# Stream mixing by 32x32 tiles on TensorE, with one reordering on ScalarE and one on VectorE

## The reference, cut to what matters

```python
x = x + attention(layernorm(x))
x = x + autocorrelation(layernorm(x), ctx, ctx)        # FFTs over the 128 tokens, 9 best lags per channel
x = x + ffn(layernorm(x))

def ffn(x):                                            # n = 4 streams of C = 256 channels per token
    x_norm = x * rsqrt(mean(x * x) + RMS_EPS)
    H_res  = sinkhorn(x_norm @ W_res.T + H_res_base)   # a 4x4 matrix per token, 50 iterations, tau 0.1
    H_pre  = softmax(x_norm @ W_pre.T + H_pre_base);  H_post = softmax(x_norm @ W_post.T + H_post_base)
    H_res  = (1 - g) * I + g * H_res                   # g = sigmoid(gate)
    y      = einsum('btnc,btn->btc', x_streams, H_pre) @ W_branch
    return einsum('btij,btjc->btic', H_res, x_streams) + einsum('btc,btn->btnc', y, H_post)
```

## Time and profile before

| | us |
|---|---|
| three runs | 1181.81, 1184.62, 1187.58 |
| the profiled execution | 1182.99 |
| its span, first to last instruction | 1181.20 |
| TensorE busy | 1020.6 (86% of the span) |
| VectorE busy | 904.2 (77%) |
| ScalarE busy | 611.9 (52%) |
| GpSimd busy | 488.6 (41%) |
| mean granted clock of TensorE | 0.941 of 2.4 GHz |

### The profile page before, as it was taken

How to read it: one execution, slowest core, us unless ns; L and a number is a source line. 1 busy time by engine, 2 the same in 40 slices (tenths; PEclk the granted TensorE clock), 3 DMA queues, 4 the chain that set the end, 5 groups by cost and what they waited for, 6 DMA issues and landing times. The chain is left out here.

```text
span 1181.2 us, 23560 instructions
## 1 busy us (share of the span) xinstructions
PE 1020.6 (86%) x7954; PEld 775.4 (66%) x7954; DVE 904.2 (77%) x2830; ACT 611.9 (52%) x1801; POOL 488.6 (41%) x721
## 2 busy tenths in 40 slices
PE   5899999999999999999966999999998988722538
PEld 4687777877777777778755677777676665411325
DVE  6786687666876667866554787788999999899993
ACT  6644455444555435554455677777766654310314
POOL 0723443333433334332342666667666653202212
PEclk9999999999999999999979999999999999755769
DMA  9111011111011110111032222243223311119406
GB/s 377 47 61 44 33 45 60 60 42 49 29 60 60 56 45 19 60 60 44 26 110 107 90 77 94 86 125 94 76 80 97 110 41 41 41 45 358 115 1 179
DMA packets 47236, 95.73 MB, mean 81 GB/s; under 512 B 5952, under 2 KB 30400, under 8 KB 47168
## 3 DMA queue, kind: packets, MB, share of 16 engines
q1 hardware_dynamic: 46880, 94.65, 24.1%
q10 hardware_dynamic: 288, 0.26, 0.1%
HBM read 64.48 MB, written 27.26 MB: 78 GB/s over the span
## 5 line engine op out<-in xcount | busy, mean ns | idle before, releaser
L696 POOL TENSOR_TENSOR prob_G<-prob_G,rl 128x512 f32<-128x512 f32 x96 | 99.7, 1040 | 246.5 <-DVE rl L570 246.5
L436 ACT ACTIVATE prob_G<-prob_G,negm 128x128 f32<-128x128 f32 x384 | 148.8, 390 | 83.9 <-DVE negm L512 83.9
L291 PE MATMUL ps_qkv<-w_hi,xT_hi 128*128 128x512 f32 x384 | 156.4, 407 | 12.5 <-DVE prob_G L581 8.6
L292 PE MATMUL ps_qkv<-w_lo,xT_hi 128*128 128x512 f32 x384 | 151.2, 394 | 0.0
L293 PE MATMUL ps_qkv<-w_hi,xT_lo 128*128 128x512 f32 x384 | 151.1, 393 | 0.0
L365 PE MATMUL ps_qkv<-wo_hi,aT_hi 128*128 128x512 f32 x256 | 107.8, 421 | 0.0
L366 PE MATMUL ps_qkv<-wo_lo,aT_hi 128*128 128x512 f32 x256 | 101.9, 398 | 0.0
L367 PE MATMUL ps_qkv<-wo_hi,aT_lo 128*128 128x512 f32 x256 | 101.9, 398 | 0.0
L508 DVE TENSOR_TENSOR prob_G<-ps_s,mask 128x512 f32<-128x512 f32 x96 | 64.9, 676 | 44.3 <-PE ps_s L274 43.8
L291 PEld LDWEIGHTS ps_qkv<-w_hi,xT_hi 128*128 128x128 f32 x384 | 72.9, 190 | 37.8 <-issue 15.9
L537 DVE TENSOR_TENSOR xT_lo<-ps_t,xT_hi 128x512 fp32r<-128x512 f32 x16 | 11.1, 691 | 94.9 <-ACT xT_hi L475 94.9
(11 more groups left out here) (290 smaller groups left out, 2763.5 us busy)
## 6 DMA issues: line engine op xcount, KB each, us to landing
xin<-in_x SPq DMA_DIRECT2D x16, 512.0 KB, 3.4
xres<-in_x SPq DMA_DIRECT2D x16, 512.0 KB, 5.5
x<-xres SPq DMA_DIRECT2D x16, 512.0 KB, 2.7
c_xin<-x SPq DMA_DIRECT2D x16, 512.0 KB, 5.5
c_cin<-in_ctx SPq DMA_DIRECT2D x16, 512.0 KB, 4.8
c_b_xres<-x SPq DMA_DIRECT2D x16, 512.0 KB, 3.3
rows_x<-c_row SPq DMA_DIRECT2D x64, 128.0 KB, 2.3
m_xm<-rows_x SPq DMA_DIRECT2D x16, 512.0 KB, 8.1
```

Source lines behind the costliest of these rows:

```text
L291: nc.tensor.matmul(ps_qkv[:, n, :], xT_hi[:, k, :], w_hi[:, k, cols], start=k == 0, stop=False)
L292: nc.tensor.matmul(ps_qkv[:, n, :], xT_hi[:, k, :], w_lo[:, k, cols], start=False, stop=False)
L436: r = nc.scalar.activation(prob(g)[:, j, :], prob(g)[:, j, :], ACT.Exp, bias=negm[:, h:h + 1], accum_out=lsum[:, h:h + 1])
L696: nc.gpsimd.tensor_tensor(prob(g), prob(g), rl[:, g * GROUP:(g + 1) * GROUP].rearrange("p (j o) -> p j o", o=1).to_broadcast([P, GROUP, T] ...
```

## The change

- **Tiles.** A group of mixing is now eight tokens and four streams, 32 lanes. `branch_part` and `row_part` become sixteen matmuls each of 32x32, on the four row strips and four column strips of the array, still with 256 moving columns. `post_diag` and `diag` have 128 elements per lane and row where they had 128 and 512, one GpSimd instruction per row each. A PSUM bank belongs to a row strip.
- **Constants.** `select` needs sixteen matmuls instead of four, with a quarter of the columns each; its matrices `sel` grow from 256 KB to 1 MB, and `place` (256 KB) and `fold_own` are new. `copies` is one instruction of 128 lanes.
- **Transfers.** A finished row goes out to `rows_x` in one transfer instead of four, in its natural order; it is loaded back in four transfers per row (32 lanes, pieces of 1 KB) instead of one (128 lanes of 4 KB). `TOKENS` is 8.
- **ScalarE's order.** Chain a's coefficients are copied and its rows 0 to 4 taken out ahead of chain b's first logs, row 5 behind them; chain c's second logs stand behind row 9 instead of row 8; rows 11 and 12 are now shared with VectorE too (`SHARED` = 11).
- **Bodies 8 to 14.** The first half of the residual is taken between the fourth and fifth pick (`residual_amid`). In bodies 8 to 13 the squares of the row move from the body's end to between the two key spectra of the next body (`squares_late`).

```diff
+        def residual_amid(b):
+            return isinstance(b, int) and 8 <= b < B - 1
+        def squares_late(b):
+            return isinstance(b, int) and 8 <= b < B - 2
@@ autocorrelation, sync
-                    for g in range(NS):
-                        lanes = slice(g * W, (g + 1) * W)
-                        sp.dma_start(rows_x[b - 2].rearrange("(j t) g c -> g t j c", j=NS)[g],
-                                     row[par][lanes, 0:D].rearrange("p (j c) -> p j c", j=NS)).then_inc(row_out[par], 16)
+                    sp.dma_start(rows_x[b - 2], row[par][:, 0:D]).then_inc(row_out[par], 16)
@@ autocorrelation, scalar
+            def row_squares(m):
+                act.wait_ge(x2_bias_done, m + 1)
+                nc.scalar.activation(squares[:], x2[:], ACT.Square, bias=x2_bias[:], scale=1.0 / D ** 0.5,
+                                     accum_out=x2_var[:]).then_inc(x2_sq_done, 1)
                 if near:
                     key_spectrum(0, f_b)
+                    if isinstance(b, int) and squares_late(b - 1):
+                        row_squares(b - 1)
                     key_spectrum(1, f_c)
@@ autocorrelation, vector
                         beside(b, 4)
+                        if i == KD // 2 - 1 and residual_amid(b):
+                            residual_begun()
+                            residual(0)
@@ mixing, sync
+            sp.dma_start(place_sb[:], place).then_inc(const_in, 16)
             sp.dma_start(sel_sb[:], sel).then_inc(const_in, 16)
             sp.dma_start(fold_sb[:], fold).then_inc(const_in, 16)
+            sp.dma_start(fold_own_sb[:], fold_own).then_inc(const_in, 16)
-                    sp.dma_start(xm[n][:], rows_x[n]).then_inc(rows_in[group(chain)], 16)
+                    for r in range(NS):
+                        sp.dma_start(xm[n][strip(r), :, :],
+                                     rows_x[n].rearrange("(r g t) (j c) -> r (t j) g c", r=NS, g=NS, j=NS)[r]).then_inc(rows_in[group(chain)], 16)
@@ mixing, tensor
                 for g in range(NS):
-                    r = nc.tensor.matmul(p_sel[:, g, 0:chain.n * N2], sel_sb[:, g, :],
-                                         coef[:, rows, :].rearrange("p b k -> p (b k)"), start=True, stop=True)
+                    for j in range(NS):
+                        r = nc.tensor.matmul(p_sel[:, g, 0:chain.n * NS], sel_sb[:, g * NS + j, :], coef[:, rows, j:N2:NS],
+                                             start=j == 0, stop=j == NS - 1)
-                        pe.wait_ge(rows_in[group(c)], 32 * c.n)
+                        pe.wait_ge(rows_in[group(c)], 16 * (NS + 1) * c.n)
-                    nc.tensor.matmul(stream_out(n, g), d[:, g * NS:(g + 1) * NS, :].rearrange("p i t -> p (i t)"),
-                                     xm[n][:, g, :], start=False, stop=True).then_inc(mix_ps, 1)
+                for r in range(NS):
+                    for g in range(NS):
+                        nc.tensor.matmul(bank(n, r)[strip(g), 0:C], d[strip(r), g, :, :].rearrange("p t i -> p (t i)"),
+                                         xm[n][strip(r), g, :], start=False, stop=True).then_inc(mix_ps, 1)
@@ mixing, scalar
-                for j in range(2 if chain is one_c else NS):
-                    dst, src = spread_at(chain, j)
-                    nc.scalar.activation(dst, src, ACT.Copy).then_inc(spread_done, 1)
+                dst = spread[:, chain.first_row:chain.first_row + chain.n, :].rearrange("p b (g i) -> p g b i", g=NS)
+                src = p_sel[:, :, 0:chain.n * NS].rearrange("p g (b i) -> p g b i", i=NS)
+                nc.scalar.activation(dst, src, ACT.Copy).then_inc(spread_done, 1)
+            copies(one_a)
+            take_out(0, one_a.n - 1)
             logs(one_b, FIRST_LOGS + 1, FIRST_LOGS + BLOCK_LOGS)
-            copies(one_a)
-            take_out(0, one_a.n)
+            take_out(one_a.n - 1, one_a.n)
@@ mixing, gpsimd
-                    for g in range(NS):
-                        folded, own = by_token(n, g, 1)
-                        nc.gpsimd.tensor_tensor(diag[n % RING][:, g * NS:(g + 1) * NS, :], folded, own, ALU.mult).then_inc(diag_done, 1)
+                    folded, own = by_token(n)
+                    nc.gpsimd.tensor_tensor(diag[n % RING][:, :, :, :], folded, own, ALU.mult).then_inc(diag_done, 1)
```

More of the change, by code:

```diff
@@ L21 @@
 C = D // NS
+TOKENS = 8
 NLOG = NS * NS + 2 * NS
@@ L1372, in body @@
                 chain_logs(b, 2)
[L1373 to L1376, removed]
+                if far and not squares_late(b):
+                    row_squares(b)
             def ending():
@@ L1548, in body @@
                             nc.vector.tensor_scalar(wgt[:, i, :], wgt[:, i, :], wrec[:, i:i + 1], None, ALU.mult).then_inc(w_done, 1)
[L1549 to L1552, removed]
+                if far and not residual_amid(b):
+                    residual_begun()
                     residual(0)
@@ L1714, in _, with mixing_phase @@
             iterations(pool, body)
-def mixing_phase(nc, row0, rows_x, rows_y, facts, chains, gate, sel, fold, out):
+def mixing_phase(nc, row0, rows_x, rows_y, facts, chains, gate, sel, place, fold, fold_own, out):
     with ExitStack() as ctx:
@@ L1765, in group, with strip, by_token, bank @@
             return chains.index(chain)
[L1767 to L1778, removed]
[L1779 to L1789 removed]
+        def strip(k):
+            return slice(k * W, (k + 1) * W)
+        def by_token(n):
+            wide = [P, NS, TOKENS, NS]
+            folded = fold_sb[:, :].rearrange("p (o t u) -> p o t u", o=1, u=1).to_broadcast(wide)
+            own = spread[:, n, :].rearrange("p (g o i) -> p g o i", g=NS, o=1).to_broadcast(wide)
+            return folded, own
+        def bank(n, r):
+            return p_out[(NS * n + r) % BANKS]
+        def part_out(n, r):
+            return bank(n, r)[:, 0:C]
         @block.sync
@@ L1862, in _ @@
+            pe.wait_ge(const_in, 64)
             pe.wait_ge(own_step, 2)
-            for g in range(NS):
-                r = nc.tensor.matmul(p_sel[:, g, 0:B], sel_sb[:, g, :], own_mean[:, :], start=True, stop=True)
-            r.then_inc(mean_ps, 1)
+            for r in range(NS):
+                last = nc.tensor.matmul(p_sel[:, r, 0:B], place_sb[:, r, :], own_mean[:, :], start=True, stop=True)
+            last.then_inc(mean_ps, 1)
             select(one_a)
             for n in range(B):
+                branch_part(n)
@@ L2064, in rope_tables, with selections @@
     return np.stack([cc * scale, ss * scale, cc, ss], 1).astype(np.float32)
+def selections():
+    r, g, t = np.meshgrid(np.arange(NS), np.arange(NS), np.arange(TOKENS), indexing="ij")
+    token = (r * NS + g) * TOKENS + t
+    sel = np.zeros((P, NS, NS, P), np.float32)
+    place = np.zeros((P, NS, P), np.float32)
+    for k in range(NS):
+        sel[token, g, k, (r * TOKENS + t) * NS + k] = 1
+        place[token, r, (g * TOKENS + t) * NS + k] = 1
+    eye = np.eye(TOKENS, dtype=np.float32)
+    own = np.eye(NS, dtype=np.float32)[None, :, None, :, None] * eye[None, None, :, None, :]
+    return {
+        "sel": sel.reshape(P, NS * NS, P),
+        "place": place,
+        "fold": np.tile(np.repeat(eye, NS, 0), (NS, 1)),
+        "fold_own": np.broadcast_to(own, (NS, NS, TOKENS, NS, TOKENS)).reshape(P, NS, TOKENS),
+    }
 def constants():
```

161 lines of the change are left out of this document (76 added, 85 removed).

## The result

| | before | changed |
|---|---|---|
| median of 8 runs each, us | 1184.26 | 1194.84 |
| lowest to highest, us | 1180.25 to 1187.68 | 1191.69 to 1197.76 |
| profiled span, us | 1181.2 | 1191.4 |
| ratio, 95% interval | 1 | 1.0096, 1.0080 to 1.0112 |

The changed kernel is 1.0% slower: 1194.8 us where 1182.6 was forecast and 1190.5 was the end of the range.

The account below looks back on a forecast made before the run. VectorE was taken to bound the kernel until 1145.3 us, then TensorE. Terms -3.7 + 6.3 - 2.45 - 1.5 + 0.5 - 0.6 - 0.6 = -2.05 us, put on the median 1184.62, gave 1182.6 us, range 1176.5 to 1190.5.

Parts of the forecast that it names:

- the stall: Mixing phase: VectorE stands from 1087.35 until ScalarE has evicted chain a's rows, to 1093.7; +6.3 us.
- When the rows come: Start of mixing: by SyncE's issues and a 3.8 us landing, chain a's rows are in at 1083, before at 1078.02.
- The byte sum of the prediction: Load of chain a's rows: 14.8 + 3.3 = 18.1 us of bytes from about 1066, so 1084.5.
- ScalarE's pace: Chain a's evictions ahead of chain b's first logs: five more rows at 1.77 us each, 8.9 us.
- Rival C: Row loads back up: issues cost 0.75 us, rows in at 1092.5, VectorE stands 15.8 us; 1192.1 us, chance 0.11.
- Chain c's wait: Mixing: VectorE's wait for chain c's first logs goes, as only one row stands ahead of them; -2.45 us.
- GpSimd: Mixing: shorter diagonals slow VectorE's iterations less, -1.5 us; longer post diagonals cost +0.5 us.
- The phase boundary: Before mixing: one transfer for four shortens VectorE's idle 1.02 us; -0.6 us (0 to -1).
- The bodies: Bodies 8 to 14: moved squares bring the first key spectrum earlier, 0.1 us in each of six bodies; -0.6 us.
- The tail: After chain b: faster tiled rows, longer selections, stores binding at the end; -3.7 us (-5 to 0).
- D: Row parts: the tiles don't overlap, four at a time, a row takes 4 us; 1200 us or over, chance 0.04.
- rival B: Selections: TensorE's clock falls to half, chain c's takes 7.4 us, the tail's gain is used up; 1186.3 us, chance 0.20.

Follow-up runs that it names:

- the second combined run: Changed kernel with ScalarE's order as before, loads of chains b and c held back, selections by 4 matmuls and stores by half rows: 0.9876, 1169.7 us.

## Why the prediction was wrong

In spans the forecast was -2.05 us and the result +10.2. The step that failed is the load of chain a's rows, a term whose bytes were given no price, and behind it TensorE's pauses, which were in no term; the stall they make was put at 6.3 us and is 14.0. Step by step:

- **When the rows come: the step that failed first.** I took SyncE's pace and the shortest landing, 3.8 us, for 1083. SyncE's pace was right (the last load of chain a issued at 1080.1); the landing was 8. I bounded the bytes by the stores' 265 GB/s, saw the difference as small, and took the lower end. Loads by strips run at 244, and the queue then grows behind SyncE, which offers 128 KB every 0.475 us, 276 GB/s. I had the right resource and put its price at nothing: 4.6 us. The byte sum of the prediction ends at 1084.1 and not at its 1084.5 (1066 + 18.1); with 244 GB/s in it, it gives 1085.4, where the rows came at 1087.6 on the same scale. So 2.4 of the 4.6 us is that rate, and the rest isn't told apart.
- **The rule I didn't weigh.** I named the piece size, and a run refuted it. The Trainium skill (SBUF — State Buffer, Door 1: The DMA port swizzle) says that a transfer's rate goes by how many of 16 ports its partitions reach, that 32 partitions in a row reach 8, and puts that at about 218 GB/s. An estimate from its 218 for the four fifths of the bytes that go by strips and the 412 of the run with 4 KB loads for the rest is 240 GB/s; the changed kernel's trace has 244, so it agrees. Its 218 is no limit here, though: stores by strips ran at 252 to 288 GB/s. The rule was about this very change.
- **ScalarE's pace.** I took 1.77 us for each of five rows, 8.9 us. Each took 1.57, but with TensorE's pause the five took 11.4 from 1090.41. ScalarE's wait at that pause is 2.54 of it; its other waits for TensorE, 1.0 us together, are what its faster evictions save. The pause was in no term: I counted the instructions of a selection, and for the rows only their array time. Rows, first eviction and pause give 4.6 + 0.4 + 2.5 of the 7.7 us by which the stall was too short.
- **Rival C** had the end nearly right (1192.1) for another reason: issues did not slow down (0.432 us each, 1.379 at most), the landings did. Its point of decision, rows at 1091, was too late, since it knew nothing of the pauses.
- **Chain c's wait**, -2.45: right, it is gone. **GpSimd**, -1.0 net: right in sign; where no stall disturbs the reading (the second combined run) chain b's last logs are 75.4 us behind the phase's start, where before it was 79.7 with the 2.45, so it is -1.8. In the changed kernel itself the same subtraction leaves -2.5, with three of the six diagonals built while VectorE stands.
- **The phase boundary**, -0.6: the wait fell from 1.02 to 0.33 us, right. **The bodies**, -0.6: nothing that can be measured, inside its bounds.
- **The tail**, -3.7, came out as +0.6. The tiles did overlap: a shared row of two parts takes 1.37 us (evictions at 1181.27 and 1182.64), so D fell. The last selection started 17.5 us behind chain b's logs, as forecast (17.4), with some luck: rows 7 and 8 came 2.0 us apart, TensorE being at half clock, and row 9 in 1.57, not 1.77 each. Then the sizes failed: it took 5.08 and not 3.7 us, with the clock falling to 0.72 (half of rival B), and the row part behind it ran at half clock, so the first shared row was out 25.1 us behind the logs and not 22.6. From there the stores took 13.8 us and not 12.0: SyncE's 18 issues stood 0.66 us apart and not 0.475. I had written that the stores bind, and still took a saving for tiles that are faster than the stores: at 252 GB/s a row of 524 KB takes 2.1 us, where TensorE took 2.57 before, and the longer selection leaves the store queue empty (62 GB/s from 1175 to 1180).

## What to carry to other kernels

When a change cuts a transfer into several, ask on which partitions each one ends, and not only how long its pieces are: the same 128 KB with the same issues ran at 239 GB/s on 32 partitions, and at 283 and waiting for its issuer on 128. A work order that puts the bound engine's inputs behind a load is only as good as that load, so price it at the load's worst bound and not its best. And a faster stage pays only down to the pace of the next: here that of the stores and of SyncE, which issues them, over 2 us per row where TensorE delivered a row in 1.37.

## What was not expected of the hardware

- A transfer between DRAM and a strip of 32 partitions keeps the DMA engines fully busy (share 1.07 and 1.11) at 239 to 244 GB/s; over 128 partitions they moved 412. Stores by strips ran at 252 GB/s with a share of 0.83 in the changed kernel and at 288 with 0.95 in the run with short selections, over 128 partitions at 325 with 0.94.
- TensorE stood 2.0 to 5.8 us at a time on "issue" in runs of 32x32 instructions while the DMA engines were fully busy with loads (share over 1), two or three times in chain a's six rows; 0.8 and 1.2 us at a share of 0.85; and 0.4 to 0.7 us in the same rows with no loads queued. The kernel before has a quarter as many instructions per row, and the view of its waits names issue for no matmul of this phase.
- A part of sixteen tiles of 32x32 by 256 columns takes 1.17 us at half clock (1.2 GHz); two of them 1.37 at 2.4 GHz. In the last selection, 32 narrow instructions without a gap, the clock fell (0.97, 0.72, 0.60 in the windows before, in and behind it). With 8 instructions it stayed at 1.00 in the second combined run, but fell to 0.50 from 1170 to 1172 us in the run with the short selections alone, so the length of the selection doesn't settle it, and it stays open.
